# Two starts and one short attention of a perceiver kernel, reordered: one query tile ahead of the rest, softmax by halves, fewer filler matmuls

## The reference

```python
x = x + L0_xattn(layernorm(x), ctx, mask)    # 16 heads, 6272 keys, keys past a length masked
x = x + L0_attn(layernorm(x))                # 16 heads of width 8, 64 x 64, causal, rotary
x = x + L0_moe(layernorm(x))                 # 8 experts, the best 2 of each token
x = x + L1_xattn(layernorm(x), ctx)          # 16 heads against ctx, no mask, then 64 x 64 on its own result
x = x + L1_delta(layernorm(x))
x = x + L1_ffn(layernorm(x))

# L0_attn
scores = einsum('bhsd,bhtd->bhst', q, k) / sqrt(8) * tril(ones)
scores = where(scores == 0.0, -inf, scores)
out = einsum('bhst,bhtd->bhsd', softmax(scores), v).reshape(B, S, 128) @ wo.T
```

## Time and profile before

| | us |
|---|---|
| median of 3 runs | 431.19 |
| the runs | 433.72, 430.61, 431.19 |
| the profiled execution | 431.47 |
| its span, first to last instruction | 429.1 |
| start, to the first maximum of layer 0 | 26.7 |
| flash loop of layer 0 and its end | to 182 |
| short attention | about 187 to 202 |
| mixture of experts | about 205 to 219 |
| first maximum of layer 1 | 226.1 |

### The profile page before, as it was taken

How to read it: one execution, slowest core, us unless ns; L and a number is a source line. 1 busy time by engine, 2 the same in 40 slices (tenths; PEclk the granted TensorE clock), 3 DMA queues, 4 the chain that set the end, 5 groups by cost and what they waited for, 6 DMA issues and landing times.

```text
span 429.1 us, 12061 instructions
## 1 busy us (share of the span) xinstructions
PE 397.4 (93%) x4811; PEld 315.2 (73%) x4811; DVE 319.2 (74%) x865; ACT 284.7 (66%) x557; POOL 202.5 (47%) x125
## 2 busy tenths in 40 slices
PE   6998999999999999999988989999999999899975
PEld 3966677777776778888974667667677778788964
DVE  2498888888887887645749989999888887543544
ACT  3247888788787886643336879888988896533240
POOL 1086897898875551001000657879656660030000
PEclk9599999999999999999999999999999999999989
DMA  8769797989999997960002999999999999600000
GB/s 318 291 191 154 149 174 128 181 136 213 229 180 214 224 180 142 418 258 0 5 2 40 179 172 178 194 189 183 173 214 192 191 196 192 257 2 2 5 0 5
DMA packets 186423, 68.13 MB, mean 159 GB/s; under 512 B 181360, under 2 KB 181888, under 8 KB 185472
## 3 DMA queue, kind: packets, MB, share of 16 engines
q1 hardware_dynamic: 186080, 66.32, 76.1%
q10 hardware_dynamic: 288, 1.05, 0.7%
HBM read 21.90 MB, written 0.03 MB: 51 GB/s over the span
## 4 chain that ended last, share of the span: by engine, by line
PE 36%; DVE 29%; ACT 9%; issue 8%; DMA 8%; POOL 5%; SPq 2%; DVEq 0%; POOLq 0%; ACTq 0%
DVE probs L586 13%; PE ps L498 9%; DMA probsT<-halves 7%; PE ps L466 7%; PE ps L721 4%; ACT probs L530 4%; POOL halves L562 4%; DVE probsT L615 3%; ACT halves L537 3%; SPq L414 2%; DVE U L604 2%; PE ps L1118 2%; PE ps L478 2%; PE ps L1021 2%; DVE den L599 2%
## 5 line engine op out<-in xcount | busy, mean ns | idle before, releaser
L562 POOL TENSOR_TENSOR halves<-probs,halves 128x896 f16<-128x896 f32 x67 | 126.5, 1892 | 81.7 <-ACT halves L537 80.9
L466 PE MATMUL ps<-ctxT_parts,GT_parts 128*128 128x512 f16 (+1 forms) x672 | 145.4, 353 | 10.8 <-DVE negmax L586 9.7
L498 PE MATMUL ps<-ctxN,probsT 128*128 128x128 f16 x2352 | 149.3, 219 | 5.4 <-DMA probsT<-halves 2.9
L498 PEld LDWEIGHTS ps<-ctxN,probsT 128*128 128x128 f16 x2352 | 139.3, 98 | 19.8 <-issue 4.9
L530 ACT ACTIVATE probs<-probs,shifted 128x896 f32<-128x896 f32 x112 | 115.5, 1031 | 12.6 <-DVE shifted L591 12.4
L466 PEld LDWEIGHTS ps<-ctxT_parts,GT_parts 128*128 128x128 f16 x672 | 60.2, 98 | 63.0 <-DVE negmax L586 14.5
L537 ACT CAST halves<-probs 128x896 f16<-128x896 f32 x92 | 84.9, 922 | 0.1
L586 DVE CUSTOM_DVE_ANT_0 probs<-ps,zero,negmax 128x896 f32<-128x896 f32 x56 | 67.4, 1204 | 1.3 <-PE ps L466 1.3
L586 DVE CUSTOM_DVE_ANT_0 probs<-ps,maskb,negmax 128x896 f32<-128x896 f32 x56 | 67.4, 1204 | 1.2 <-POOL halves L562 0.7
L604 DVE SCALAR_TENSOR_TENSOR U<-U,alpha,ps 128x128 f32<-128x128 f32 x112 | 38.3, 342 | 32.3 <-PE ps L498 32.2
L527 ACT ACTIVATE alpha<-negmax 128x1 f32<-128x1 f32 x96 | 28.2, 294 | 41.9 <-DVE negmax L586 41.1
(11 more groups left out here) (346 smaller groups left out, 360.2 us busy)
## 6 DMA issues: line engine op xcount, KB each, us to landing
moe<-in_ctxT SPq DMA_DIRECT2D x7, 448.0 KB, 7.8
moe<-in_mask SPq DMA_DIRECT2D x6, 448.0 KB, 10.8
moe<-in_gateT SPq DMA_DIRECT2D x2, 1024.0 KB, 9.1
moe<-in_upT SPq DMA_DIRECT2D x2, 1024.0 KB, 10.7
moe<-in_downT SPq DMA_DIRECT2D x2, 1024.0 KB, 12.6
moe<-in_fir_long SPq DMA_DIRECT2D x1, 2048.0 KB, 10.9
probsT<-halves SPq DMA_TRANSPOSE x92, 4.6
wv<-in_wv SPq DMA_DIRECT2D x2, 512.0 KB, 4.9
```

The lines of the kernel that those rows point to most:

```text
L466: ins = pe.matmul(ps[:, 2 * b + h, 0:width], GT_parts[:, g_part, r * P:(r + 1) * P], ctxT_parts[:, keys:keys + width], start=(g_part == 0 ...
L498: ins = pe.matmul(ps[:, bank, 0:D], probsT_parts[:, b, p_part, k * P:(k + 1) * P], ctxN_parts[:, at:at + D], start=(p_part == 0 and c_part ...
L562: eng.tensor_tensor(halves_of(L, n)[:, 1, :], probs[:, n % BUFS, :], halves_of(L, n)[:, 0, :], ALU.subtract).then_inc(lower_of(L, n)[0], 1)
```

## The change

It changes the order of work in three places, and a few counts.

1. **Start of layer 0.** DVE normalises as soon as x is there; the exponent -0.5 of the powers comes from a tile that POOL fills (`pows`) and no longer from `cst`. PE has one 512-column matmul less before, 1 filler instead of 2 after the turn, 2 instead of 5 before the fold, 7 instead of 5 between fold and bound, 8 instead of 12 after the bound. ACT takes chunk 5 of the channel maxima from DVE. The scale's write is put behind the square on DVE. ACT writes the first chunk's upper part in two halves, and DVE's lower halves wait for one each. POOL makes the first half of the first mask chunk before its power and the second half after the first chunk is complete.
2. **Both long attentions begin with one tile.** The parts of GT are made for tile 0 first (128 columns), then for tiles 1 to 3 (384 columns); `score(0)` waits for the first, `score(1)` for both. The lower part of tiles 4 to 7 is made at step 1. In layer 1 the fold itself is split: tile 0 goes to bank 6, the first half of the fold stands before `score(0)`, the second between `score(0)` and `score(1)`.
3. **The short attention by halves.** The keys are spread over 4 blocks, not 16; the score matmuls use 32 of the partitions and 256 columns each, four in all, and each half of the head pairs goes through mask, maximum, exponential (the maximum is now ACT's bias), sum and product by itself. The product with the values is made transposed, with the values as weights, so that the copy and the turn behind it fall away. Fillers: 22 instead of 24, and none before the probabilities' copy. WARM[1] is 0.

The diff, changed lines only eight columns of indentation taken off (left out: the constants' table, the tiles' shapes, the same exponent in `norm_pool`, the place of the scale's write on DVE, the counts of some semaphores, and the removed lines of the short attention and of the later fold, which the listing above has):

```diff
@@ -40,10 +40,11 @@
+G_READY, G_COPIED = {0: 1, 1: 3, 2: 6}, {0: 1, 1: 4, 2: 7}
-WARM = [0, 2, 6, 6, 6, 6]
+WARM = [0, 0, 6, 6, 6, 6]
@@ -500,7 +499,13 @@
+    if L == 1:
+        fold_half_pe(pe, 1, xnT, 0)
+    pe.wait_ge(sem("g_copied"), G_COPIED[L])
+    if L == 1:
+        fold_half_pe(pe, 1, xnT, 1)
+    pe.wait_ge(sem("g_copied"), G_COPIED[L] + 1)
@@ -690,7 +694,7 @@
-    pool.tensor_tensor(bound[:, L, 4:5], bound[:, L, 3:4], C("power"), ALU.pow).then_inc(sem("bound_root"), 1)
+    pool.tensor_tensor(bound[:, L, 4:5], bound[:, L, 3:4], pows[:, 0:1], ALU.pow).then_inc(sem("bound_root"), 1)
@@ -729,7 +733,7 @@
-        stay_warm(pe, 2, 2)
+        stay_warm(pe, 2, 2 if i else 1)
@@ -739,7 +743,7 @@
-        stay_warm(pe, 6, 5)
+        stay_warm(pe, 6, 2)
@@ -753,19 +757,26 @@
...
+        stay_warm(pe, 6, 7)
...
+        fold_half_pe(pe, i, src, half)
+def fold_half_pe(pe, i, src, half):
+    for k in range(PAIRS // 2):
+        bank = 6 if i == 1 and half == k == 0 else 4 + half
+        for par_ in range(2):
+            for side in range(2):
+                rows, col = slice(side * S, (side + 1) * S), k * P + par_ * S
+                ins = pe.matmul(ps[rows, bank, col:col + S], w_qk[par_][:, 4 * half + k, rows], src[:, 0:S],
+                                start=True, stop=True)
+        if bank == 6:
+            ins.then_inc(sem("g_ready"), 1)
+    ins.then_inc(sem("g_ready"), 1)
@@ -797,28 +808,32 @@
-    dve.wait_ge(sem("g_ready"), 2 * i + 1)
-    if i == 2:
-        dve.tensor_scalar(GT[:, 0:4, :].rearrange("p r c -> p (r c)"), ps[:, 4, :], DK ** -0.5, None,
-                          ALU.mult).then_inc(sem("g_copied"), 1)
+        for tiles in (slice(0, P), slice(P, 4 * P)):
+            first = tiles.start == 0
+            bank = 6 if i == 1 and first else 4
+            dve.wait_ge(sem("g_ready"), G_READY[i] + (i == 1 and not first))
+            seq(dve.tensor_scalar(GT_parts[:, 0, tiles], ps[:, bank, tiles], g_scale[:, i:i + 1], None,
+                                  ALU.mult))
+            g_lower_dve(dve, i, tiles, bank)
+            if first:
+                descale_dve(dve, seq, i, kappa)
-    seq(dve.tensor_scalar(GT_parts[:, 0, 0:4 * P], ps[:, 4, :], g_scale[:, i:i + 1], None, ALU.mult))
-    g_lower_dve(dve, i, 0)
-    descale_dve(dve, seq, i, kappa)
-    if i == 0:
-        g_lower_dve(dve, i, 1)
-def g_lower_dve(dve, i, half):
-    if half == 1:
+    dve.wait_ge(sem("g_ready"), G_READY[i])
+    dve.tensor_scalar(GT[:, 0:4, :].rearrange("p r c -> p (r c)"), ps[:, 4, :], DK ** -0.5, None,
+                      ALU.mult).then_inc(sem("g_copied"), 1)
+def g_lower_dve(dve, i, cols, bank):
+    if bank == 5:
-    cols = slice(half * 4 * P, (half + 1) * 4 * P)
-    dve.scalar_tensor_tensor(GT_parts[:, 1, cols], ps[:, 4 + half, :], g_scale[:, i:i + 1],
-                             GT_parts[:, 0, cols], ALU.mult, ALU.subtract).then_inc(sem("g_copied"), 1)
+    at = cols.start % (4 * P)
+    dve.scalar_tensor_tensor(GT_parts[:, 1, cols], ps[:, bank, at:at + cols.stop - cols.start],
+                             g_scale[:, i:i + 1], GT_parts[:, 0, cols], ALU.mult,
+                             ALU.subtract).then_inc(sem("g_copied"), 1)
-    act.activation(probs[:, c // 4, :], ctxT_raw[:, c * CK:(c + 1) * CK], ACT.Abs,
+    act.activation({1: probs[:, 0, :], 4: probs[:, 1, :], 5: probsT[:, 0, :]}[c], ctxT_raw[:, c * CK:(c + 1) * CK], ACT.Abs,
@@ -834,10 +849,13 @@
+        channel_sum_act(act, 5)
-        act.activation(ctxT_parts[:, 0:CK], ctxT_raw[:, 0:CK], ACT.Copy,
-                       scale=ch_scale[:]).then_inc(sem("ctxT_upper"), 1)
-    act.wait_ge(sem("g_ready"), 2 * i + 2)
+        for half in range(2):
+            keys = slice(half * HALF, (half + 1) * HALF)
+            act.activation(ctxT_parts[:, keys], ctxT_raw[:, keys], ACT.Copy,
+                           scale=ch_scale[:]).then_inc(sem("ctxT_upper"), 1)
+    act.wait_ge(sem("g_ready"), G_READY[i] + (2 if i == 1 else 1))
@@ -951,15 +969,14 @@
-    for _ in range(12):
+    for _ in range(11):
-    stay_warm(pe, 6, 12)
-    pe.wait_ge(sem("g_copied"), 1)
+    stay_warm(pe, 6, 8)
@@ -980,26 +997,30 @@
...
+    pe.wait_ge(sem("w_qk_ready"), 4)
+    for half in range(2):
+        for hh in range(2):
+            dims = slice((2 * hh + half) * DD, (2 * hh + half + 1) * DD)
+            ins = pe.matmul(ps[hh * S:(hh + 1) * S, 3 + half, 0:4 * S], aqT[dims, 0:S], kexp[dims, :, :],
+                            start=True, stop=True)
+        ins.then_inc(sem("a_given"), 1)
+    stay_warm(pe, 6, 22)
+    for half in range(2):
+        pe.wait_ge(sem("a_probs"), half + 1)
+        for k in range(2):
+            j = 2 * half + k
+            ins = pe.transpose(ps[:, half, k * P:(k + 1) * P], sm[:, 2 * j:2 * j + 2, :].rearrange("p a t -> p (a t)"),
+                               ident)
+        ins.then_inc(sem("a_given"), 1)
+    for half in range(2):
+        pe.wait_ge(sem("a_pcopied"), half + 1)
+        for q in (half, 2 + half):
+            for r in range(2):
+                pr = 2 * q + r
+                hh, j = pr // 4, pr % 4
+                ins = pe.matmul(ps[q * DD:(q + 1) * DD, 5, 0:S], vblk[:, pr, :, :].rearrange("p r c -> p (r c)"),
+                                PT[:, j, hh * S:(hh + 1) * S], start=(r == 0), stop=(r == 1))
...
@@ -1052,8 +1073,6 @@
-    fold_q_pe(pe, 1, xnT)
-    pe.wait_ge(sem("g_copied"), 3)
@@ -1264,15 +1283,17 @@
+    pool.memset(vblk[:], 0.0).then_inc(sem("vblk_cleared"), 1)
+    pool.memset(pows[:], -0.5)
-    loaded(pool, "cst")
+    pool.wait_ge(sem("cleared"), 3)
@@ -1292,9 +1313,12 @@
+    pool.wait_ge(sem("ld_mask0"), 16)
+    pool.tensor_scalar(maskb[:, 0:HALF], mask_raw(0)[:, 0:HALF], 0.0, MASKED, ALU.is_equal, ALU.mult)
-    mask(0)
+    pool.tensor_scalar(maskb[:, HALF:CK], mask_raw(0)[:, HALF:CK], 0.0, MASKED, ALU.is_equal,
+                       ALU.mult).then_inc(sem("mask_ready"), 1)
@@ -1377,10 +1400,16 @@
-    act.wait_ge(sem("a_shifted"), 1)
-    act.activation(sm, sm2, ACT.Exp, scale=float(1.0 / np.sqrt(AD))).then_inc(sem("a_exp"), 1)
-    act.wait_ge(sem("a_given"), A_GIVEN["pturned"])
-    act.copy(PT.rearrange("p j c -> p (j c)"), ps[:, 4, :]).then_inc(sem("a_pcopied"), 1)
+    for half in range(2):
+        act.wait_ge(sem("a_max"), half + 1)
+        for k in range(4):
+            r = 4 * half + k
+            ins = act.activation(sm[:, r, :], sm2[:, r, :], ACT.Exp, bias=smx[:, r:r + 1])
+        ins.then_inc(sem("a_exp"), 1)
+    for half in range(2):
+        act.wait_ge(sem("a_given"), A_GIVEN["pturned"] + half)
+        act.copy(PT[:, 2 * half:2 * half + 2, :].rearrange("p j c -> p (j c)"),
+                 ps[:, half, 0:2 * P]).then_inc(sem("a_pcopied"), 1)
@@ -1473,11 +1502,12 @@
-    loaded(dve, "x", "cst")
+    loaded(dve, "x")
+    loaded(dve, "cst")
-    flash_dve(dve, 0)
+    flash_dve(dve, 0, {1: partial(g_lower_dve, dve, 0, slice(4 * P, 8 * P), 5)})
@@ -1496,25 +1526,17 @@
...
+    dve.wait_ge(sem("vblk_cleared"), 1)
+    for r in range(2):
+        ins = dve.tensor_tensor(vblk[:, r::2, r, :].rearrange("p q (a d) -> p q a d", a=2),
+                                ps[:, 1, 0:D].rearrange("p (q r a d) -> p q r a d", q=4, r=2, a=2)[:, :, r],
+                                C("half").unsqueeze(1).unsqueeze(3).broadcast_to([P, 4, 2, AD]), ALU.mult)
+    seq(ins)
...
+    dve.tensor_tensor(kexp, ps[:, 2, P:P + S].unsqueeze(1).broadcast_to([P, DH, S]),
+                      C("head8").unsqueeze(2).broadcast_to([P, DH, S]), ALU.mult).then_inc(sem("a_made"), 1)
@@ -1522,12 +1544,23 @@
...
+    for half in range(2):
+        rs = slice(4 * half, 4 * half + 4)
+        dve.wait_ge(sem("a_given"), A_GIVEN["scores"] + half)
+        sc = ps[:, 3 + half, 0:4 * S].rearrange("p (h t) -> p h t", h=4)
+        seq(dve.scalar_tensor_tensor(sm[:, rs, :], sc, 0.0, C("later").unsqueeze(1).broadcast_to([P, 4, S]),
+                                     ALU.is_equal, ALU.max))
+        seq(dve.scalar_tensor_tensor(sm2[:, rs, :], sm[:, rs, :], NEVER, sc, ALU.mult, ALU.add))
+        dve.tensor_reduce(smx[:, rs], sm2[:, rs, :], AX, ALU.max, negate=True).then_inc(sem("a_max"), 1)
+    for half in range(2):
+        rs = slice(4 * half, 4 * half + 4)
+        dve.wait_ge(sem("a_exp"), half + 1)
+        seq(dve.tensor_reduce(ssum[:, rs], sm[:, rs, :], AX, ALU.add))
+        seq(dve.reciprocal(ssum[:, rs], ssum[:, rs]))
+        dve.tensor_tensor(sm[:, rs, :], sm[:, rs, :], ssum[:, rs].unsqueeze(2).broadcast_to([P, 4, S]),
+                          ALU.mult).then_inc(sem("a_probs"), 1)
...
+    dve.tensor_copy(oT[:], ps[:, 5, 0:S].unsqueeze(1).broadcast_to([P, 2, S])).then_inc(sem("a_made"), 1)
```

87 lines of the change are left out of this document (19 added, 68 removed).

## The result

The changed kernel took a median of 423.97 us (422.58 to 426.19, 4 runs) beside 432.44 us for the kernel before (430.61 to 433.72, 4 runs): ratio 0.9862, 95% interval 0.9827 to 0.9896. Two further series of the same kernel gave 425.01 and 424.55 us with ratios 0.9873 (0.9834 to 0.9912) and 0.9863 (0.9828 to 0.9897). So by the ratios it is 1.3 to 1.4% faster, 5.5 to 6 us. The plain differences of the medians are 8.5, 5.9 and 5.1 us; the first ratio on record isn't the quotient of its two medians, which is 0.9804, and the 8.5 rests on four executions of each. The forecast was 4.35 us less, 427.1. The profiled execution took 426.19 us, the slowest of the first four, with a span of 424.4 us against 429.1: a difference of 4.7.

The account below looks back on a forecast made before the run. It took PE's own queue, at 1.2 GHz, to bound the start, and fillers ending last to bound the short attention. Terms 1.65 + 0.1 + 2.1 + 0.5 = 4.35 off 431.47 gave 427.1 us, range 424.4 to 430.4.

Parts of the forecast that it names:

- Start, fold: Layer 0's start: fold begins at 11.8 instead of 14.69, the bound's matmul at 19.05, 1.9 us earlier.
- The first rival: Layer 0's start: clock stays high through the first fold, at most 2.1 us more gained, 425.5 us; chance 0.22.
- The term of 1.65: Layer 0's loop: third maximum begins at 27.7 instead of 29.36, a gain of 1.65 us.
- Start, first tile: Layer 0's start: first score 0.8 us earlier still, then DVE's 384-column parts delay the maxima; third maximum at 27.7.
- Does the loop keep its lead?: Long loops of 56 steps: a loop that begins earlier ends earlier by as much.
- Second normalisation: Ahead of the short attention: two fillers less gain 0.1 us, range 0 to 0.47.
- the bound from below: Second normalisation: gain could be 0, since ACT's copies of the folded weights must be done before the next product.
- Short attention: Short attention by halves with 22 fillers for 24: gain of 2.1 us, range 1.4 to 2.6.
- the rival of the four score pieces at once: Short attention: the score pieces run together, half of 1.08 us goes, 426.6 us; chance 0.08.
- Layer 1's start: Layer 1's first steps: first score at 223.0 instead of 224.62, 0.5 us left at the third maximum; bounds 0 and 1.3.
- The rival on the other side: Short attention and experts: clock falls, experts run at half of it, costing up to 12 us, 439 us; chance 0.05.
- the two rivals of higher gain: High clock through layer 0's first fold, 425.5 us, chance 0.22; four score pieces at once, 426.6 us, chance 0.08.

Follow-up runs that it names:

- e2: Changed kernel with DVE waiting for x and the constants together before it normalises: 428.08 us, ratio 0.9933 to the kernel before.
- e3: Kernel before with only the short attention by halves added: 426.66 us, ratio 0.9901 to the kernel before.
- e1: Changed kernel unaltered, measured again: 425.01 us, ratio 0.9873 to the kernel before.
- e9: Changed kernel unaltered, measured again in a later series: 424.55 us, ratio 0.9863 to the kernel before.
- e4: Changed kernel with both long attentions beginning with four tiles at once and layer 1's fold whole before the first score: 425.19 us, ratio 0.9883.
- e8: Changed kernel with both score pieces of an output half reading the same 32 partitions: 424.98 us in its one run.
- e10: Changed kernel with queries copied ahead of chunk 2's maximum, 14 opening matmuls for 11, 3 and 18 fillers in the short attention: 424.44 us, ratio 0.9870.
- e7: Changed kernel with 14 opening matmuls for 11 and 5 fillers for 2 behind the query product: 424.23 us, ratio 0.9844.
- e5: Changed kernel with fewer fillers: 3 for 7 before the bound, 3 for 6 and 18 for 22 around short attention scores, 10 for 14 in tail: 425.21 us.
- e6: Changed kernel with queries copied ahead of chunk 2's maximum, 3 and 18 fillers in the short attention, 10 in the tail: 423.12 us, ratio 0.9835.
- e12: Changed kernel with the edits of e10 and e11 together: 424.24 us, ratio 0.9854 to the kernel before.
- e11: Changed kernel with 4, 2 and 1 fillers in PE's three gaps ahead of the tail's 14 fillers: 424.03 us, ratio 0.9868.

## Why the prediction was right, and where its terms were off

The forecast of 427.1 lies 2 to 3 us above the three medians; two of them are inside its range of 424.4 to 430.4, and the first, 423.97, is 0.4 below its low end. The four terms read 1.65, 0.1, 2.1 and 0.5. The high end was added up too high: with nothing from the start and layer 1 and 1.4 from the attention it is 431.47 - 1.4 = 430.1. In the profiled pair the sum came out at 4.78 against 4.35, and that this is so near is in part luck: start and short attention gave 0.8 and 0.7 more than forecast, and the tail, which no term named, took 1.45 back.

*Start, fold.* Begin 11.8 forecast, 11.76, 11.72 and 11.66 measured: the chain from chunk 2's landing over its maximum to the copy was right for the changed kernel. It was wrong as the account of the kernel before, where five fillers and not the copy stood last ahead of the fold (e2); their removal and the faster product by themselves give 2.0 of the 2.9 (e2), and the prediction never priced it. The gap before the turn, put at about 0.5, was 1.01, 0.28 and 0.21 in the three profiles. The bound at 19.05 forecast came at 18.47 in one profile and near 16.8 in two. The first rival, a clock that stays high through the first fold, chance 0.22, is what happened in those two and in part in the first; its price of at most 2.1 more was right (19.05 - 16.8 = 2.2), also in that the bound then waits for the operand. What the prediction missed is that the course isn't a property of either kernel: e3, with the old start, has the high clock in its fold too. The term of 1.65 was worked out for a fold at half clock. With that nearly met, in the profiled pair (4.04 and 3.63), the start gained 29.36 - 26.89 = 2.47; e3 against e1 and e9, whose folds all take 2.31, gives 26.89 - 25.3 = 1.6. That this is the forecast's figure is luck, since e3 had its query product at half clock and e1 and e9 had not.

*Start, first tile.* The third maximum was put at 19.05 + 8.65; measured 8.37 to 8.58 behind the bound with the split, and 8.27 to 8.42 without (before, e3, e4). So the split was priced at a net loss of 0.24 and is worth 0 to a loss of 0.1 or 0.2 (8.41 and 8.42 against 8.42 and 8.41 where the bound's matmul takes 0.43, 8.27 against 8.37 where it takes 0.28 to 0.39): what is gained at the first maximum is paid back by the parts of 384 columns.

*Does the loop keep its lead?* Yes: third maximum to x takes 154.78 before and 154.68, 154.72 and 154.75 in the changed kernel. Layer 1's loop keeps it less exactly, 159.05 before and 158.82, 158.74 and 159.18.

*Second normalisation.* 0.1 forecast, 0 measured (e3 against the changed kernel: 7.25 both): ACT's copies hold the product, as the bound from below said.

*Short attention.* 2.1 forecast, 2.79 measured, and this is the term that was mis-sized: outside its own range of 1.4 to 2.6. Step by step: scores' begin 0.32 (0.25 forecast), the score group to the fillers' start 0.41 (0 forecast), two fillers fewer 0.44 (0.47), from the fillers' end to x 3.92 to 2.30, 1.62 (0.2 + 0.55 + 0.65 = 1.40). The 0.41 is the rival of the four score pieces at once, which had 0.08. It was priced by columns per instruction, as if pieces could share PE only where they write different output halves; e8 shows that the 32 partitions they read are what counts. By the Trainium skill ("TensorE: Matmul & The Clock Gate", Part 3: Packing small matmuls) tiles on different row strips run at once; and a short contraction by itself saves nothing, as the same page's table under "Why this matters for your kernels" has it. Both halves of that rule agree with the runs: 0.66 on four strips, 1.08 on two, as the 128 partitions took the earlier trace rows.

*Layer 1's start.* 0.5 forecast, 0.64 measured, against 1.5 that the first score itself gained (22.36 to 20.85 behind x of the short attention); e4 shows it for this part alone.

*The rival on the other side*, a long fall in the short attention and the experts, didn't come. The granted clock in 40 slices of the changed kernel's span:

```profile
PEclk9699999999999999999999999999999999999969
```

It is at 9 in each slice from the third to the 38th, and 1.00 from 181 to 223, where the short attention and the experts lie. A smaller relative did, in a place that the prediction didn't name: the low stretch of the tail, which costs 1.3 to 1.7 in five of the profiles (changed, e4, e8, e9, e10) and nothing in the kernel before, where it falls on the same fillers but later; nor in e1, e2, e3 and e7. That turns give less cover than other matmuls wasn't tested apart.

*Sum.* With 1.6 for the start, 1.6 + 0 + 2.79 + 0.64 = 5.0, and the executions ordered by their clock say 5.0; with the 2.47 of the profiled pair it would be 5.9 before the tail's loss of 1.45. So the agreement is no proof of the 1.6. The ratios say 5.5 to 6. That the changed kernel keeps the high clock more often fits this; it isn't shown to be the whole of the rest, and which of its parts does it, the runs don't separate. Of the two rivals of higher gain (0.22 and 0.08) the one on the clock came true in part and the one on the score pieces nearly whole (0.41 of its 0.5), and they add; the forecast had given the combination only the low end of its range.

## What to carry to other kernels

Price small matmuls by the partitions that they read as well as by their columns: four pieces on four strips of 32 took 0.66 us where the same four on two strips took 1.08. Where one program's executions spread by 1%, read the granted clock of each before a gain is put down to an edit, and compare short stretches between fixed points (x to x) that agree to 0.02 us over profiles, not end times: the long loops alone differed by up to 1.6 us here. Before a gain is shared out between two parts of a change, take each away by itself: here either of two gave most of the fold's move. Fillers that end just ahead of their operand at full clock are the bound at half clock, and fewer of them can cost more later than they give.

## What the runs showed of the hardware

- The weights of the opening matmuls of 512 columns are loaded every 0.43 us up to 5.43 (changed kernel: 2.45, 2.88, 3.30 and so on), which is 512 columns at 1.2 GHz, though the clock column says 1.00 from 0 to 5. So the column, and with it the mean clock, misses this low stretch. The eleven took 4.20, 4.87 and 4.88 us in the three profiles of the changed kernel.
- TensorE's clock fell and rose at different points of the same program (fold of 3.63, 2.31 and 2.31 us in three profiles of the changed kernel), and in e5 it fell in the last stretch behind 2.3 us of idle time and stayed low until near 422.
- With PE idle for 0.72 us or not at all before the fold, TensorE stayed at 2.4 GHz through the start (e6, e7, e10, e12). With 1.18 to 1.35 us idle there it fell in the profiles of the changed kernel, e1, e4, e5, e8 and e9, each time between 12.2 and 14.5, and didn't fall in e11's. In the kernel before, e2 and e3, with 1.78 to 2.33 us idle before the turn, it fell earlier, between 8.2 and 10.9.
- Four score pieces of 256 columns took 0.66 us on four strips of 32 partitions (changed kernel, e3) and 1.08 on two (e8).
- The Trainium skill ("TensorE: Matmul & The Clock Gate", Part 1: The HAM clock gate) states that the monitor behind the clock runs freely and isn't reset when a kernel starts, so that the point of change varies from run to run. By that rule, these profiles agree: the same code had its fold at either level.
